# Sixteen attention heads: both value products moved out of the loop over score blocks into runs of 32 matmuls, and half of the layer norm's transpose copies moved to VectorE

## The chip, the cores and the metric

One Trainium2 chip, all 8 cores. Every core runs the same program on its own part of the data, and no core waits for another. The metric is the device time in microseconds of the slowest core. Names of engines: PE is TensorE (its matmuls; PEld its weight loads), DVE is VectorE, ACT is ScalarE, POOL is GpSimd, SP is SyncE.

## The reference, cut to what matters

```python
xn = _layernorm(x)                                  # x: (4, 2048, 2048)
w = (xn @ W.T).reshape(B, T, 16, 128)               # 16 heads of 128
q = _rms_norm(w, g1); k = _rms_norm(w, g2); v = _rms_norm(w, g3)
att = einsum('bhid,bhjd->bhij', q, k) / sqrt(128)
score = softmax(att, axis=-1) + softmax(att, axis=-2)
y = einsum('bhij,bhjd->bihd', score, v)
s = y @ W
g = _silu(_ffn(xn))          # silu(xn@w_gate*s_gate) * (xn@w_up*s_up) @ w_down * s_down
x = x + s * g
```

A core computes 1024 of the 2048 output rows of one batch entry, and needs all 2048 rows as keys and values. Queries, keys and values are one matrix (`rn`, the normalised projection), so the scores are symmetric but for the scales.

## The kernel before, in words

The program is a list of operations for each engine, written out in Python by `Sched.add` (`A` in the code). An engine works off its list in the order written. Each operation counts up a semaphore lane, and `M` reads the count so far, so that a later operation can wait for it. All engines but PE also wait, before each operation, until their own operation before it has ended; an operation of the list may hold many instructions, and between those nothing is waited for. Barriers divide the program into stages.

Stage 1, projection (0 to about 437 us). For each of 16 blocks `tb` of 128 rows: `emit_ln_tr` computes the layer norm (ACT and small DVE operations), `emit_tr` transposes the block by matmuls with the identity matrix, in four groups `grp` of four 128x128 pieces, which alternate between PSUM banks 4 and 5 (L233), and copies each group to SBUF on ACT (L242, L247); `emit_wproj` multiplies by W in two halves of 32 matmuls of 512 columns (L265), and each half is squared by ACT (L276), summed by DVE (L282), turned into a factor by ACT (L288, L292) and scaled into `rn` by DVE (L299). The order in the list is: layer norm of `tb`, projection of `tb-1`, transposes of `tb`.

Stage 2, heads (about 438 to 1625 us), the loop over `h` from L329. For each of 16 heads:

- ACT makes three small vectors of exponentials of the running shift `nMu` (`eMb`, `eMf`, `eNg`: L330, L334, L337).
- PE transposes the head's slice of `rn` (L346, 16 pieces in 4 groups), ACT copies it to `rnT` (L358), DVE scales it to `rnTq` (L362) and makes `vv2`, the values scaled by `eMf`, in 16 instructions (L365).
- The loop over 16 row blocks `rb` (L400). `a_block` computes scores (L383): two matmuls of 512 columns for `rb` below 8, and for `rb` from 8 on two for the low half and two for the high half. ACT takes the exponential of 1024 columns into `Ei[rb]` (L419), and from `rb` 8 on of the high half into a scratch tile (L425), which is needed for its sum alone. PE adds `vv2[rb]` times `Ei[rb]` to the first value product, Y1 (L443, two matmuls).
- In the same loop PE works on the second value product, Y2, of the head before (`pend`): L405, two matmuls a round, which read `Ei[rb]` of that head. There is one `Ei`, so the exponential of the round, which overwrites `Ei[rb]`, waits for them (the list `ew`, L416 to L418). At the end DVE adds Y1 and Y2 (L457) and stores the head (L460).
- After the loop: a logarithm on ACT (L463), the column sums (L470, 64 matmuls of one column), eight small DVE operations (L478 to L490) that end in the reciprocals `rS` and the column factors `fbf`, then `vv1`, the values scaled by `rS`, as 16 single operations (L495), and the factors spread over all partitions: eight small matmuls (L502), a copy to a row (L508), two matmuls (L512, L514), a copy (L518), and the product with Y1 (L521).

After the last head, Y2 of head 15 is done by itself, 32 matmuls in a row (L545), and added and stored (L554, L556).

Stage 3 (1625 us to the end): multiplication by W (L585), then the two feed-forward passes (L658, L664, L723) with weights that stream from memory.

PSUM in stage 2: Y1 in columns 0 to 1023, score buffers at 1024 and 3072, the high half at 3072, Y2 at 2048.

Of the kernel before, what the change touches and what calls it, by code (L numbers as in the profile page):

```python
# [51 lines left out]
def build(debug=False):  # L52
# [95 lines left out]
    A = sch.add  # L148
# [34 lines left out]
    trv_done = [0, 0, 0, 0]  # L183
# [41 lines left out]
    def emit_tr(tb):  # L225
        bi, bj = tb % 3, tb % 2
        for grp in range(4):
            bank = 4 + (grp % 2)
            def tfn(t, tb=tb, bj=bj, grp=grp, bank=bank):
                last = None  # L230
                for kk in range(4):
                    k = grp * 4 + kk
                    last = t.matmul(  # L233
                        PS[:, bank * 512 + kk * 128: bank * 512 + (kk + 1) * 128],
                        xn_t[bj][:, 128 * k:128 * (k + 1)], ident[:, :],
                        start=True, stop=True)
                return last
            A("T", tfn, 1, [("S", ln_xn_mark[bi]), ("S", trv_done[2 * (grp % 2)])])
            tg = M("T")
            if tb < 8:  # L240
                def vfn(v, tb=tb, grp=grp, bank=bank):
                    return v.copy(  # L242
                        xnT_lo[:, 4 * grp:4 * (grp + 1), 128 * tb:128 * (tb + 1)],
                        PS[:, bank * 512:(bank + 1) * 512])
            else:
                def vfn(v, bj=bj, grp=grp, bank=bank):
                    return v.copy(  # L247
                        xnT_t[bj][:, 4 * grp:4 * (grp + 1), :],
                        PS[:, bank * 512:(bank + 1) * 512])
            A("S", vfn, 1, [("T", tg), ("T", xnTt_user[bj] if tb >= 8 else 0)])  # L250
            trv_done[2 * (grp % 2)] = M("S")
        tr_done[bj] = M("T")
        trv_all_t[tb] = M("S")

    def emit_wproj(tb):
        for fh in range(2):
            slot = (2 * tb + fh) % 2
            pofs = slot * 1024
            for k in range(16):
# [11 lines left out]
                kw = [("S", trv_all_t[tb]), ("V", pw_user[slot])] if k == 0 else []  # L271
# [52 lines left out]
    prev_tcs = 0  # L324
    prev_tft = 0
    prev_y1c15 = 0
    pend = None
    trv = [0, 0]
    for h in range(NH):  # L329
        A("S", lambda s: s.activation(eMb[:, :], nMu[:, :], AF.Exp, bias=0.0,  # L330
                                      scale=consts[:, C_NEG1:C_NEG1 + 1]), 1,
          [("V", prev_s1war), ("T", prev_tcs)])
        semb = M("S")
        A("S", lambda s: s.activation(eMf[:, :], nMu[:, :], AF.Exp, bias=0.0,  # L334
                                      scale=consts[:, C_NEG1:C_NEG1 + 1]), 1)
        semf = M("S")
        A("S", lambda s: s.activation(eNg[:, :], nMu[:, :], AF.Exp, bias=0.0,  # L337
                                      scale=1.0), 1)
        seng = M("S")
        for grp in range(4):  # L340
# [24 lines left out]
        A("V", lambda v, h=h: [v.tensor_scalar_mul(  # L365
            vv2[:, rb, :], rn[:, rb, 128 * h:128 * (h + 1)],
            eMf[:, rb:rb + 1]) for rb in range(16)][-1], 1,
          [("S", semf), ("T", prev_y1c15)])
        vvv2 = M("V")

        def a_block(rb, lo, ws):
            if rb < 8:
                pofs = 1024 if rb % 2 == 0 else 3072
                nr = (0, 1)
            elif lo:
                pofs, nr = 1024, (0, 1)
# [12 lines left out]
            A("T", afn, 1, ws)  # L389
            return M("T")  # L390

        amark_lo = {}
        amark_hi = {}
        amark_lo[0] = a_block(0, True, [("V", vq)])
        amark_lo[1] = a_block(1, True, [("V", vq), ("V", prev_fbcV)])
        exp_mark = {}
        exp_done = {}
        y1c_mark = {}
        cur_y2c = {}
        for rb in range(16):  # L400
            if pend is not None:
                def yfn(t, hp=pend["h"], rb=rb):
                    last = None
                    for n in range(2):
                        last = t.matmul(  # L405
                            PS[:, 2048 + 512 * n:2048 + 512 * (n + 1)],
                            vv1[:, rb, :], Ei[:, rb, 512 * n:512 * (n + 1)],
                            start=(rb == 0), stop=(rb == 15))
                    return last
                ws = [("V", pend["vv1m"][rb])]  # L410
                if rb == 0:
                    ws += [("V", pend["fbcV"]), ("S", trv[0])]
                A("T", yfn, 1, ws)
                cur_y2c[rb] = M("T")
            slot = 1024 if (rb >= 8 or rb % 2 == 0) else 3072
            ew = [("T", amark_lo[rb])]  # L416
            if pend is not None:
                ew.append(("T", cur_y2c[rb]))  # L418
            A("S", lambda s, rb=rb, slot=slot: s.activation(  # L419
                Ei[:, rb, :], PS[:, slot:slot + 1024], AF.Exp,  # L420
                bias=nMu[:, rb:rb + 1], scale=1.0,
                accum_out=S1[:, rb:rb + 1]), 1, ew)
            exp_mark[rb] = M("S")
            if rb >= 8:
# [15 lines left out]
            def y1fn(t, rb=rb):  # L440
                last = None
                for n in range(2):
                    last = t.matmul(PS[:, 512 * n:512 * (n + 1)],  # L443
                                    vv2[:, rb, :],
                                    Ei[:, rb, 512 * n:512 * (n + 1)],
                                    start=(rb == 0), stop=(rb == 15))
                return last
            y1w = [("S", exp_mark[rb]), ("V", vvv2)]
            if rb == 0:
                y1w.append(("V", prev_scY1))  # L450
            A("T", y1fn, 1, y1w)
            y1c_mark[rb] = M("T")
            if rb >= 8 and rb <= 14:
                amark_hi[rb + 1] = a_block(rb + 1, False,
                                           [("S", exp_done[rb])])
            if pend is not None and rb == 15:
                A("V", lambda v: v.tensor_tensor(  # L457
                    scY2[:, :], scY1[:, :], PS[:, 2048:3072], ALU.add), 1,
                  [("T", cur_y2c[15])])
                A("V", lambda v, hp=pend["h"]: v.tensor_scalar_mul(  # L460
                    y_st[:, hp, :], scY2[:, :], gv[:, 3:4]), 1)
                prev_scY2 = M("V")
# [13 lines left out]
        A("T", csfn, 1, [("S", semb), ("S", exp_done[15]), ("V", prev_scY2)])  # L476
        tcs = M("T")
        A("V", lambda v: v.tensor_sub(nM[:, :], nMu[:, :], nM[:, :]), 1,  # L478
          [("S", sln)])
        A("V", lambda v: v.tensor_scalar_min(nMu[:, :], nM[:, :], 0.0), 1)  # L480
        A("V", lambda v: v.tensor_copy(cs_sb[:, :], PS[:, 2560:2568]), 1,
          [("T", tcs), ("S", seng)])
# [383 lines left out]
```

How the kernel before makes its waits and increments, by code:

```python
        def emit(eng_name, eng):  # L779
            last_wait = {k: 0 for k in Sched.LANES}
            done = {k: 0 for k in Sched.LANES}
            for (fn, inc, waits, lane) in sch.ops[eng_name]:
                ws = list(waits)
                if lane != "T" and done[lane] > last_wait[lane]:
                    ws.append((lane, done[lane]))
                for (we, wv) in ws:
                    if wv > last_wait[we]:
                        eng.wait_ge(sems[we], wv)
                        last_wait[we] = wv
                if fn is None:
                    inst = eng.nop()
                else:
                    inst = fn(eng)
                if inc:
                    inst.then_inc(sems[lane], inc)
                done[lane] += inc
```

## Time and profile before

| | us |
|---|---|
| two runs of the kernel | 3539.60 and 3624.77 |
| their median | 3582.19 |
| the profiled execution, device time | 3539.33 |
| its span, slowest core (core 1) | 3537.8 |
| spans of the other cores | 3520.1 to 3534.3 |
| mean granted TensorE clock, all cores | 0.884 to 0.887 of 2.4 GHz |

The profile is of one execution, on its slowest core. The span runs from the core's first to its last instruction; the device time is 1.5 us longer. The two medians of the dies are 3533.1 and 3529.8 us. The clock takes two values in the records of all eight cores, 0.5 and 1.0 of full speed (1.2 and 2.4 GHz). The page divides the span into 40 slices of 88 us; stage 2 fills slices 5 to 18. The durations of matmuls are modelled, and reach a little past the start of the next.

### The profile page before, as it was taken

The page shows a single profiled execution, that of the slowest core. Times are in us where ns is not written, and L with a number is a line of the kernel's source. Part 1 is how long each engine was busy: PE and PEld are TensorE (multiplying, and loading weights), DVE is VectorE, ACT ScalarE, POOL GpSimd, SP SyncE. Part 2 cuts the span into 40 slices and gives each one's busy share as a digit, 9 for nine tenths or more (in the row PEclk, how much of TensorE's full clock was granted, in tenths as well). Part 3 has the DMA queues.
Part 4 walks back from the last instruction along what each step waited for, and adds up shares of the span by engine and source line. Part 5 has one row for each costly group of instructions (what it writes and reads, how often), then busy time and mean ns, then how long its engine had stood idle before and what let it go on. Part 6 is the DMA issues. An engine that isn't in the chain of part 4 may idle for free.

```text
span 3537.8 us, 30050 instructions; the slowest of 8 cores (3520.1 to 3537.8 us)
## 1 busy us (share of the span) xinstructions
PE 2445.0 (69%) x11176; PEld 1014.5 (29%) x11176; DVE 587.4 (17%) x1171; ACT 821.4 (23%) x1306; POOL 138.2 (4%) x222
## 2 busy tenths in 40 slices
PE   2777755445554454544989999775768999976565
PEld 0333311111111111111434444322223444422222
DVE  0222211221111221111112222001002122200101
ACT  2555454444444344440000011000000101100000
POOL 0000000000000000000000000010110000001010
PEclk9888888878888778886989999998898999989898
DMA  7111000000000000005034433355554334345543
GB/s 155 42 42 48 1 1 0 1 1 0 1 1 1 1 0 1 0 1 95 36 156 168 164 143 143 143 179 197 182 202 167 143 143 160 126 177 179 202 178 143
DMA packets 56305, 329.20 MB, mean 93 GB/s; under 512 B 4961, under 2 KB 4961, under 8 KB 43873
## 3 DMA queue, kind: packets, MB, share of 16 engines
q0 software_dynamic: 48384, 285.23, 23.1%
q1 hardware_dynamic: 7778, 42.05, 3.4%
q8 instruction: 91, 1.49, 0.2%
q14 instruction: 52, 0.43, 0.0%
HBM read 197.24 MB, written 12.58 MB: 59 GB/s over the span
## 4 chain that ended last, share of the span: by engine, by line
PE 48%; DMA 23%; ACT 15%; issue 7%; DVE 5%; ACTq 0%; DVEq 0%; POOLq 0%; POOL 0%; SPq 0%; PEldq 0%
DMA wdb<-wd_in 19%; PE PS L658 13%; PE PS L664 12%; ACT Ei L419 9%; PE PS L265 7%; PE PS L383 5%; PE PS L405 4%; ACT escr L425 3%; PE PS L585 3%; DVE vv L495 2%; DMA whT<-wt_in 2%; PE PS L443 2%; PE PS L470 1%; ACT rnT L358 1%; DMA ws_lo<-ws_in 1%
## 5 line engine op out<-in xcount | busy, mean ns | idle before, releaser
L723 PE MATMUL PS<-wdb,fuse 128*128 128x512 bf16 x2048 | 535.1, 421 | 273.0 <-DMA wdb<-wd_in 248.8
L383 PE MATMUL PS<-rnT,rnTq 128*128 128x512 bf16 x768 | 250.2, 414 | 405.0 <-ACT Ei L419 345.1
L658 PE MATMUL PS<-xnT_lo,wgb 128*128 128x512 bf16 x2048 | 467.5, 382 | 23.5 <-DVE outs_t L754 19.4
L664 PE MATMUL PS<-xnT_lo,wub 128*128 128x512 bf16 x2048 | 462.9, 379 | 0.0
L419 ACT ACTIVATE Ei<-PS,nMu 128x1024 bf16<-128x1024 f32 x256 | 285.0, 1113 | 445.8 <-PE PS L405 442.2
L723 PEld LDWEIGHTS PS<-wdb,fuse 128*128 128x128 bf16 x2048 | 208.9, 106 | 599.2 <-issue 429.3
L658 PEld LDWEIGHTS PS<-xnT_lo,wgb 128*128 128x128 bf16 x2048 | 201.4, 98 | 270.1 <-issue 31.6
L677 ACT ACTIVATE guscr<-PS,sgv 128x512 f32<-128x512 f32 x128 | 87.9, 687 | 797.2 <-PE PS L664 797.2
L664 PEld LDWEIGHTS PS<-xnT_lo,wub 128*128 128x128 bf16 x2048 | 200.3, 98 | 241.7
L383 PEld LDWEIGHTS PS<-rnT,rnTq 128*128 128x128 bf16 x768 | 52.6, 99 | 598.9 <-issue 598.9
L682 DVE TENSOR_SCALAR guscr<-PS,suv 128x512 f32<-128x512 f32 x128 | 96.1, 751 | 697.9 <-ACT guscr L677 697.9
L746 ACT ACTIVATE outs_t<-scrA 128x2048 f32<-128x2048 f32 x8 | 15.3, 1909 | 819.5 <-DVE scrA L736 819.5
L443 PE MATMUL PS<-Ei,vv 128*128 128x512 bf16 x512 | 164.5, 405 | 23.2 <-ACT Ei L419 23.2
L265 PE MATMUL PS<-whT,xnT_lo 128*128 128x512 bf16 x512 | 136.2, 433 | 44.2 <-DMA whT<-wt_in 36.1
L405 PE MATMUL PS<-Ei,vv 128*128 128x512 bf16 x480 | 162.1, 423 | 0.0
L457 DVE TENSOR_TENSOR scY<-scY,PS 128x1024 f32<-128x1024 f32 x15 | 18.3, 1221 | 794.4 <-PE PS L405 794.4
L736 DVE TENSOR_TENSOR scrA<-PS,sd_bc 128x2048 f32<-128x2048 f32 x8 | 18.3, 2292 | 766.8 <-PE PS L723 766.4
L425 ACT ACTIVATE escr<-PS,nMu 128x1024 bf16<-128x1024 f32 x128 | 142.5, 1113 | 12.4 <-ACT Ei L419 0.7
L265 PE MATMUL PS<-whT,xnT_t 128*128 128x512 bf16 x512 | 129.8, 421 | 8.2 <-ACT xnT_t L247 8.2
L710 POOL DMA_DIRECT2D wdb<-wd_in x128 | 91.3, 713 | 807.5 <-DMA wdb<-wd_in 643.1
L685 DVE TENSOR_TENSOR fuse<-guscr,guscr 128x512 bf16<-128x512 f32 x128 | 88.7, 693 | 13.3
L265 PEld LDWEIGHTS PS<-whT,xnT_lo 128*128 128x128 bf16 x512 | 53.8, 107 | 124.5 <-issue 79.4
(93 smaller groups left out, 1313.1 us busy)
## 6 DMA issues: line engine op xcount, KB each, us to landing
wdb<-wd_in POOLq DMA_DIRECT2D x128, 1024.0 KB, 5.3
wgb<-wg_in POOLq DMA_DIRECT2D x32, 2048.0 KB, 7.5
wub<-wu_in POOLq DMA_DIRECT2D x32, 2048.0 KB, 11.8
x_t<-x_in SPq DMA_DIRECT2D x16, 1024.0 KB, 5.2
whT<-wt_in POOLq DMA_DIRECT2D x8, 1024.0 KB, 15.6
xr_t<-x_in SPq DMA_DIRECT2D x8, 1024.0 KB, 7.2
out<-outs_t SPq DMA_DIRECT2D x8, 1024.0 KB, 4.0
ws_lo<-ws_in POOLq DMA_DIRECT2D x4, 1024.0 KB, 12.2
```

Source lines behind the costliest of these rows:

```text
L265: last = t.matmul(PS[:, pofs + 512 * n: pofs + 512 * (n + 1)], lhsT, whT[:, k, 1024 * fh + 512 * n: 1024 * fh + 512 * (n + 1)], start=(k = ...
L383: last = t.matmul(PS[:, pofs + 512 * n: pofs + 512 * (n + 1)], rnTq[:, 128 * rb:128 * (rb + 1)], rnT[:, 512 * n:512 * (n + 1)], start=True ...
L405: last = t.matmul(PS[:, 2048 + 512 * n:2048 + 512 * (n + 1)], vv1[:, rb, :], Ei[:, rb, 512 * n:512 * (n + 1)], start=(rb == 0), stop=(rb = ...
L419: A("S", lambda s, rb=rb, slot=slot: s.activation(Ei[:, rb, :], PS[:, slot:slot + 1024], AF.Exp, bias=nMu[:, rb:rb + 1], scale=1.0, accum_ ...
L425: A("S", lambda s, rb=rb: s.activation(escr[:, :], PS[:, 3072:4096], AF.Exp, bias=nMu[:, rb:rb + 1], scale=1.0, accum_out=S2[:, rb:rb + 1] ...
L443: last = t.matmul(PS[:, 512 * n:512 * (n + 1)], vv2[:, rb, :], Ei[:, rb, 512 * n:512 * (n + 1)], start=(rb == 0), stop=(rb == 15))
L585: last = t.matmul(PS[:, pofs + 512 * n:pofs + 512 * (n + 1)], lhsT, rhs_t[:, fc % 8, 512 * n:512 * (n + 1)], start=(fc == 0), stop=(fc == 15))
L658: last = t.matmul(PS[:, pg:pg + 512], wgb[wbi][:, k, 128 * ib:128 * (ib + 1)], xnT_lo[:, k, 512 * sp:512 * (sp + 1)], start=(k == 0), stop ...
L664: last = t.matmul(PS[:, pu:pu + 512], wub[wbi][:, k, 128 * ib:128 * (ib + 1)], xnT_lo[:, k, 512 * sp:512 * (sp + 1)], start=(k == 0), stop ...
L682: A("V", lambda v, col=col, pu=pu, gp=gp: v.tensor_scalar_mul(guscr2[gp][:, :], PS[:, pu:pu + 512], suv[:, col:col + 1]), 1, [("T", tgu), ...
L710: A("G", lambda g, r=r, wbi=wbi: g.dma_start(out=wdb[wbi][:, :, :], in_=wd_in[256 * r:256 * (r + 1), :].rearrange("(u p) c -> p u c", u=2) ...
L723: last = t.matmul(PS[:, pofs + 512 * n:pofs + 512 * (n + 1)], fuse[:, ic, 256 * tp + 128 * tb2:256 * tp + 128 * (tb2 + 1)], wdb[wbi][:, u, ...
```

## The change

Three things are done.

Stage 1. The copies of transposed groups 1 and 3 go from ACT to DVE (`e.tensor_copy`); groups 0 and 2 stay on ACT. PE's wait for a free bank, and the projection's wait for the transposed block, name the lane of the engine that copied.

Stage 2, the loop over row blocks. It holds only scores and exponentials. Y2 of the head before is gone from it, and with it the wait of each exponential for those matmuls; `pend` is gone, and the flush behind the last head. Y1 is gone from it too. Score blocks have two buffers in PSUM columns 0 to 2047 for `rb` below 8 (0 and 1024), and two of 2048 columns (0 and 2048) from `rb` 8 on, where low and high half are one group of four matmuls; block `rb` waits for the exponential of block `rb-2`, block 8 for that of block 7.

Stage 2, after the loop, in the order written: the three small exponentials and the logarithm (ACT), the column sums (PE, now in bank 7), `vv2` (DVE), Y1 as one run of 32 matmuls, the small DVE operations, `vv1` as one operation of 16 instructions, the eight small matmuls, the row copy, the two spreading matmuls, and Y2 of the same head as one run of 32 matmuls into columns 1024 to 2047, with the addition and the store. The next head's transposes stand behind that run on PE.

The core of the diff ("..." where lines are left out):

```diff
-    trv_done = [0, 0, 0, 0]
+    trv_done = [("S", 0), None, ("V", 0), None]
...
+            ev = "S" if grp % 2 == 0 else "V"
...
+                    return e.tensor_copy(dst, src_) if ev == "V" else e.copy(dst, src_)
+            A(ev, vfn, 1, [("T", tg), ("T", xnTt_user[bj] if tb >= 8 else 0)])
+            trv_done[2 * (grp % 2)] = (ev, M(ev))
...
-            if pend is not None:
-                def yfn(t, hp=pend["h"], rb=rb):
-                    last = None
-                    for n in range(2):
-                        last = t.matmul(
-                            PS[:, 2048 + 512 * n:2048 + 512 * (n + 1)],
-                            vv1[:, rb, :], Ei[:, rb, 512 * n:512 * (n + 1)],
-                            start=(rb == 0), stop=(rb == 15))
-                    return last
...
-            ew = [("T", amark_lo[rb])]
-            if pend is not None:
-                ew.append(("T", cur_y2c[rb]))
...
+                pofs = ((rb - 8) % 2) * 2048
+                width = 2048
+                if rb == 8:
+                    war = [("S", exp_done[6]), ("S", exp_done[7])]
...
+        A("V", vv2fn, 1, [("S", semf)])
...
+        def y1fn(t, h=h):
+            last = None
+            for rb in range(16):
+                for n in range(2):
+                    last = t.matmul(PS[:, 512 * n:512 * (n + 1)],
+                                    vv2[:, rb, :], Ei[:, rb, 512 * n:512 * (n + 1)],
+                                    start=(rb == 0), stop=(rb == 15))
+            return last
+        A("T", y1fn, 1, [("V", vvv2), ("S", sexp_all)])
...
-        for rb in range(16):
-            vw = [("T", cur_y2c[rb])] if pend is not None else []
-            A("V", lambda v, rb=rb, h=h: v.tensor_scalar_mul(
+        def vv1fn(v, h=h):
+            last = None
+            for rb in range(16):
+                last = v.tensor_scalar_mul(vv1[:, rb, :],
+                                           rn[:, rb, 128 * h:128 * (h + 1)],
+                                           rS[:, rb:rb + 1])
+            return last
+        A("V", vv1fn, 1)
...
+        A("T", y2fn, 1, [("V", vvv1)])
```

PE, the last two rounds of a head and the turn to the next, before. `L383` are scores, `L443` is Y1 (`vv_73` is `vv2`), `L405` is Y2 of the head before (`vv_72` is `vv1`), `L470` the column sums, `L502` to `L514` the factors, `L346` the transposes of the next head:

```order
L383 MATMUL PS<-rnT,rnTq 128x512 x2
L443 MATMUL PS<-Ei,vv_73 128x512 x2
L383 MATMUL PS<-rnT,rnTq 128x512 x2
L405 MATMUL PS<-Ei,vv_72 128x512 x2
L443 MATMUL PS<-Ei,vv_73 128x512 x2
L470 MATMUL PS<-eMb,Ei 128x1 x64
L502 MATMUL PS<-ident,fbf 1x128 x8
L512 MATMUL PS<-frow,ones_107 128x512
L514 MATMUL PS<-frow,ones_107 128x512
L346 MATMUL PS<-ident,rn 128x128 x16
L383 MATMUL PS<-rnT,rnTq 128x512 x4
```

PE, a whole head, after. `L379` are scores, `L439` Y1, `L492` Y2, `L418` the column sums, `L468` to `L479` the factors, `L337` the transposes of the next head:

```order
L379 MATMUL PS<-rnT,rnTq 128x512 x48
L418 MATMUL PS<-eMb,Ei 128x1 x64
L439 MATMUL PS<-Ei,vv_73 128x512 x32
L468 MATMUL PS<-ident,fbf 1x128 x8
L477 MATMUL PS<-frow,ones_107 128x512
L479 MATMUL PS<-frow,ones_107 128x512
L492 MATMUL PS<-Ei,vv_72 128x512 x32
L337 MATMUL PS<-ident,rn 128x128 x16
```

The number of matmuls in a head is the same, 48 and 32 and 32 of 512 columns; the two value products have left the stretch in which the scores stand.

ACT, the end of one projection block in stage 1, before (`L276` to `L292` the factors of the second half, `L247` the four copies of the transposed block, `L196` the next layer norm):

```order
L276 ACTIVATE PS<-PS 128x1024
L288 ACTIVATE rsv<-rmsS,consts 128x8
L292 ACTIVATE rsv<-rsv,consts 128x8
L247 CAST xnT_t_68<-PS 128x512 x4
L196 ACTIVATE xsq,lnst<-x_t_64 128x2048
```

DVE at the same place, after (`L283` the sum and `L300` the scaling of a half, `L250` the copies of groups 1 and 3, `L203` the next layer norm):

```order
L283 TENSOR_REDUCE rmsS<-PS 128x8
L300 TENSOR_TENSOR rn<-PS,rsv 128x1024
L283 TENSOR_REDUCE rmsS<-PS 128x8
L300 TENSOR_TENSOR rn<-PS,rsv 128x1024
L250 CAST xnT_t_69<-PS 128x512 x2
L203 TENSOR_SCALAR lnst<-lnst 128x1
```

On ACT two of the four copies are left at that place; on DVE the other two stand behind the scaling of the second half.

## Rows read from the trace of the kernel before

**Rows 1.** The page: the span, and the chain that ended last, by line.

```profile
span 3537.8 us, 30050 instructions; the slowest of 8 cores (3520.1 to 3537.8 us)
...
DMA wdb<-wd_in 19%; PE PS L658 13%; PE PS L664 12%; ACT Ei L419 9%; PE PS L265 7%; PE PS L383 5%; PE PS L405 4%; ACT escr L425 3%; PE PS L585 3%; DVE vv L495 2%; DMA whT<-wt_in 2%; PE PS L443 2%; PE PS L470 1%; ACT rnT L358 1%; DMA ws_lo<-ws_in 1%
```

**Rows 2.** Stage 2: length; busy PE, PEld, DVE, ACT, POOL; PEclk, DMA share, GB/s.

```profile
437.70:1625.00 1187.30, 599.50 (x3232) 223.38 (x3232) 236.37 (x752) 516.75 (x896) 0.00 (x0) 0.82 0.00 1
```

**Rows 3.** Who waited for whom: microseconds in total, times, the longest.

```profile
ACT Ei L419 <- PE PS L405: 442.2, 240, 3.9
```

**Rows 4.** Timeline, a round below 8 and two starts from 8 on: start, us, engine, line.

```profile
738.13 1.11 ACT L419 ACTIVATE Ei<-PS,nMu 128x1024 bf16<-128x1024 f32 x1 [1.75 <-PE PS L405]
...
739.48 0.59 PE L383 MATMUL PS<-rnT,rnTq 128*128 128x512 bf16 x2 [1.50 <-ACT Ei L419]
...
740.34 0.59 PE L405 MATMUL PS<-Ei,vv 128*128 128x512 bf16 x2
...
741.08 1.11 ACT L419 ACTIVATE Ei<-PS,nMu 128x1024 bf16<-128x1024 f32 x1 [1.75 <-PE PS L405]
...
751.68 1.11 ACT L419 ACTIVATE Ei<-PS,nMu 128x1024 bf16<-128x1024 f32 x1 [1.32 <-PE PS L405]
...
755.50 1.11 ACT L419 ACTIVATE Ei<-PS,nMu 128x1024 bf16<-128x1024 f32 x1 [1.32 <-PE PS L405]
```

**Rows 5.** Timeline of head 0, first exponential to the logarithm after the last.

```profile
443.89 1.11 ACT L419 ACTIVATE Ei<-PS,nMu 128x1024 bf16<-128x1024 f32 x1 [2.24 <-PE PS L383]
...
445.24 1.01 PE L383 MATMUL PS<-rnT,rnTq 128*128 128x512 bf16 x2 [0.65 <-ACT Ei L419]
...
475.01 0.22 ACT L463 ACTIVATE nM<-S 128x16 f32<-128x16 f32 x1
```

**Rows 6.** Timeline from there into head 1.

```profile
475.40 0.18 DVE L478 TENSOR_TENSOR nM<-nMu,nM 128x16 f32<-128x16 f32 x1 [30.02 <-ACT nM L463]
...
478.79 0.31 ACT L330 ACTIVATE eMb<-nMu,consts 128x16 bf16<-128x16 f32 x1 [3.56 <-DVE fcol L487]
...
479.01 1.01 PE L502 MATMUL PS<-ident,fbf 128*1 128x128 bf16 x8 [2.21 <-DVE fbf L490]
...
484.86 1.21 DVE L508 CAST frow<-PS 1x1024 bf16<-1x1024 f32 x1
486.21 0.58 PE L512 MATMUL PS<-frow,ones 1*128 1x512 bf16 x1 [6.19 <-DVE frow L508]
...
487.15 1.03 PE L346 MATMUL PS<-ident,rn 128*128 128x128 bf16 x8
...
491.66 2.69 DVE L365 TENSOR_SCALAR vv<-rn,eMf 128x128 bf16<-128x128 bf16 x16
491.70 1.87 PE L383 MATMUL PS<-rnT,rnTq 128*128 128x512 bf16 x4 [1.81 <-DVE rnTq L362]
```

**Rows 7.** Timeline of the end of stage 2.

```profile
1613.52 9.17 PE L545 MATMUL PS<-Ei,vv 128*128 128x512 bf16 x32 [1.54 <-DVE f_bc L518]
1622.86 1.22 DVE L554 TENSOR_TENSOR scY<-scY,PS 128x1024 f32<-128x1024 f32 x1 [8.16 <-PE PS L545]
```

**Rows 8.** Granted clock by stretch (PEclk, third from the end), as rows 2.

```profile
744.00:772.70 28.70, 14.89 (x58) 4.60 (x58) 1.78 (x2) 18.68 (x31) 0.00 (x0) 1.00 0.00 1
...
792.90:801.30 8.40, 5.44 (x12) 1.49 (x12) 0.00 (x0) 2.41 (x4) 0.00 (x0) 0.50 0.00 0
...
474.50:477.70 3.20, 1.74 (x64) 1.68 (x64) 0.85 (x5) 0.64 (x3) 0.00 (x0) 1.00 0.02 5
```

**Rows 9.** Timeline of stage 1, end of one block.

```profile
253.87 2.60 ACT L247 CAST xnT_t<-PS 128x512 bf16<-128x512 f32 x4
253.95 1.23 DVE L299 TENSOR_TENSOR rn<-PS,rsv 128x1024 bf16<-128x1024 f32 x1 [1.10 <-ACT rsv L292]
...
255.27 0.38 PE L233 MATMUL PS<-ident,xn_t 128*128 128x128 bf16 x4 [0.29 <-ACT xnT_t L247]
...
256.73 16.91 PE L265 MATMUL PS<-whT,xnT_t 128*128 128x512 bf16 x64 [1.07 <-ACT xnT_t L247]
```

More of the change, by code:

```diff
@@ L317, in build @@
         sch.barrier()
+    head_tail_V = 0
+    head_tail_S = 0
+    prev_csV = 0
     prev_fbcV = 0
+    prev_y2T = 0
     prev_exp15 = 0
@@ L323, in build @@
     prev_scY2 = 0
[L324 to L327, printed above, removed]
     trv = [0, 0]
     for h in range(NH):
[L330 to L339, printed above, removed]
         for grp in range(4):
@@ L440, in y1fn @@
[L440 to L462, printed above, removed]
+        sexp_all = M("S")
@@ L463, in build @@
+        A("S", lambda s: s.activation(eMb[:, :], nMu[:, :], AF.Exp, bias=0.0,
+                                      scale=consts[:, C_NEG1:C_NEG1 + 1]), 1)
+        semb = M("S")
+        A("S", lambda s: s.activation(eMf[:, :], nMu[:, :], AF.Exp, bias=0.0,
+                                      scale=consts[:, C_NEG1:C_NEG1 + 1]), 1)
+        semf = M("S")
+        A("S", lambda s: s.activation(eNg[:, :], nMu[:, :], AF.Exp, bias=0.0, scale=1.0), 1)
+        seng = M("S")
         A("S", lambda s: s.activation(nM[:, :], S1[:, :], AF.Ln,
@@ L475, in csfn, with vv2fn @@
             return last
-        A("T", csfn, 1, [("S", semb), ("S", exp_done[15]), ("V", prev_scY2)])
+        A("T", csfn, 1, [("S", semb)])
         tcs = M("T")
[L478 to L481, printed above, removed]
+        def vv2fn(v, h=h):
+            last = None
+            for rb in range(16):
+                last = v.tensor_scalar_mul(vv2[:, rb, :],
+                                           rn[:, rb, 128 * h:128 * (h + 1)],
+                                           eMf[:, rb:rb + 1])
+            return last
+        A("V", vv2fn, 1, [("S", semf)])
+        vvv2 = M("V")
+        def y1fn(t, h=h):
+            last = None
+            for rb in range(16):
+                for n in range(2):
[4 more added lines that the diff above has]
+        A("T", y1fn, 1, [("V", vvv2), ("S", sexp_all)])
+        ty1 = M("T")
+        A("V", lambda v: v.tensor_copy(cs_sb[:, :], PS[:, 3584:3592]), 1,
           [("T", tcs), ("S", seng)])
+        csV = M("V")
         A("V", lambda v: v.tensor_mul(cs_sb[:, :], cs_sb[:, :], eNg[:, 0:8]), 1)
```

171 lines of the change are left out of this document (70 added, 101 removed).

## The prediction

> **What bounds the kernel now.** I read the page first. The chain that ended last spreads over three stages [rows 1]: the feed-forward lines (wdb, L658, L664) hold the most, and the heads appear as L419, L383, L405, L425 and L443, together about a quarter. The change touches only the projection and the heads, so I cut out the heads' stage by its barriers: 1187.3 us, in which ACT is busy for 516.8, PE for 599.5, DVE for 236.4 [rows 2]. No engine is full. It is a stage of waits, and the list of waits names one above all others: ACT's exponential into Ei waits 442.2 us, 240 times, for L405, the second value product of the head before [rows 3]. That is 15 heads times 16 rounds, so every round of every head but the first.
>
> The timeline shows the ring [rows 4]. An exponential starts at 738.13; PE starts the score pair 1.35 later, when it and its sum have ended; the Y1 pair and the Y2 pair follow, the Y2 pair at 740.34; the next exponential starts at 741.08, 0.15 behind that pair's end. A round is 2.95 us, of which ACT works 1.30. From row block 8 on, with two exponentials a round, it is 3.82 (751.68 to 755.50). Sixteen rounds are 8 x 2.95 + 8 x 3.82 = 54.2 us. Head 0 has no Y2 to do, and shows the same loop without the ring: from its first exponential (443.89) to the logarithm behind the last (475.01) 31.1 us, which is 24 exponentials of 1.30 with nothing between them [rows 5]. The loop that was written to overlap two heads runs as a chain: exponential, scores, Y1, Y2, exponential.
>
> **The change, head by head.** The loop then costs what head 0 shows, and both products come behind it, in the open. I sum one head, from exponential 0 to the next head's exponential 0.
>
> 1. 24 exponentials: 31.1 us [rows 5].
> 2. Block 8 needs both buffers, so its four score matmuls start only behind exponential 7. At half clock 1.87 [rows 6], with 0.05 before (1.35 less 1.30) and 0.15 behind [rows 4]: 2.1. A matmul of 512 columns takes 0.215 at full clock (four of them from 739.48 to 740.34) and 0.43 at half (four in 1.87, two in 1.01) [rows 4 to 6]. At full clock two steps of 0.215 and a pair's 0.59 make 1.0, so the item 1.2.
> 3. To the start of Y1. Three small exponentials (0.31 for eMb and for eMf, 0.22 as the logarithm for eNg, 0.09 between them) now stand ahead of the logarithm, 1.1; the subtraction starts 0.39 behind the logarithm's start [rows 5, 6]; it and the minimum take 0.55; then vv2, 2.69 [rows 6], which was hidden beside the scores and now is in the open; 0.15 to PE (486.07 to 486.21). Together 4.9. The column sums lie beside vv2.
> 4. Y1, 32 matmuls. The flush behind the last head is that run, from a rested PE: 9.17 us [rows 7]. All at full clock it would be 31 x 0.215 + 0.38 = 7.0. I take 9.2.
> 5. From Y1 to Y2. The small DVE operations and vv1 end beside Y1: at most 3.6 (475.40 to 479.01, with the column sums in it) and, as one operation like vv2, 2.7, against 9.2. What is left is a chain that Y1 now holds up on PE: eight small matmuls (1.01 at half clock, about 0.65 at full), 0.15, row copy to L512 1.35 (484.86 to 486.21), two matmuls until PE is free again 0.94 (to 487.15), 0.45 at full [rows 6]. 2.6 at full clock, 3.45 at half. I take 2.6.
> 6. Y2: 7.0 if the clock holds over step 5, 9.2 if not. I take 7.0.
> 7. Transposes of the next head to its first score matmul: 487.15 to 491.70, 4.55, with a rested PE [rows 6]. The store of the head lies beside them on DVE (1.22 + 0.75 and gaps against 3.6). Behind a dense run the first pieces are faster: 4.3.
> 8. First pair to exponential 0: 1.01 + 0.15 [rows 5, 4] at half clock, 0.75 at full: 1.0.
>
> Sum: 31.1 + 2.1 + 4.9 + 9.2 + 2.6 + 7.0 + 4.3 + 1.0 = 62.2 us.
>
> The stage: 6.2 from its start to the first exponential (437.70 to 443.89), 15 heads of 62.2, then 56.9 (items 1 to 6), and 2.2 for addition and store (1622.86 to 1625.00) [rows 2, 5, 7]. 6.2 + 933.0 + 56.9 + 2.2 = 998.3, against 1187.3: 189 us less.
>
> **Which clock.** Items 2, 4, 5, 6 hang on it. In rounds with 58 matmuls in 28.7 us (2.0 a us) it stayed at 2.4 GHz; in rounds at a head's start with 12 in 8.4 us (1.4 a us) it stayed at 1.2 [rows 8]. The new loop issues two a 1.30 us, 1.5 a us, nearest to the second row. So scores at half clock, and Y1 starts there. For Y2 the nearest row is 474.50 to 477.70: full clock for 3.2 us in which PE did only one-column work [rows 8]. Step 5 is shorter and has ten larger matmuls in it, so Y2 starts at full clock.
>
> At half clock a pair takes 1.01 [rows 5], so scores end 0.05 + 1.01 + 0.15 = 1.21 us behind the exponential two before, under the 1.30 that the one between takes. Scores stay hidden, with 0.1 to spare.
>
> The Trainium skill has a rule that speaks against the new shape ("TensorE: Matmul & The Clock Gate", section "A second HAM failure mode: psum-queue depth-cycling"): a matmul kernel that cycles through PSUM banks with short idles between its groups swings between half and full clock, and pays for it in throughput. Rows 8 agree that both levels occur within one head. Carried to this kernel at its worst, it would leave Y1 and Y2 at half clock too; that case is priced below from rows, as the rival "half clock throughout".
>
> **The projection.** ACT's first copy stands behind the factors of the half before, and starts at 253.87; its four copies end at 256.47, the next projection starts at 256.73 [rows 9]. DVE's two copies stand behind the scaling of that half, which ends at 255.18. I have no row of DVE copying 128x512 to SBUF; 1024 columns took 1.21 in the row copy [rows 6], so half of that, 0.61, to 1.21; with a fixed part I take 0.69. Then 255.28 + 0.69, group 3 on PE (0.14 + 0.38 [rows 9]), its copy 0.14 + 0.69, and 0.26 to the projection: 257.6, 0.8 later than now. Blocks 1 to 15 pay that: 12 us. Bounds: from -9, if the copies ran beside each other and DVE's scaling were no hindrance, to +25, at 1.21 a copy.
>
> **The sum**, against the profiled execution's own time: 3539.3 - 189 + 12 = 3362 us. The median of the two runs shown is 3582.2; the profiled execution agrees with the faster of them (3539.6), and I predict for such a run.
>
> **Rivals.**
>
> - *The clock stays up in the loop.* Items 2, 4, 8 fall by 0.9, 2.2, 0.3: 3.4 a head, 55 us: 3307. For it: head 0 ran at full clock in its loop. Against it: that loop had Y1 in it.
> - *The clock falls between Y1 and Y2.* Items 5, 6, 7 rise by 0.85, 2.2, 0.25: 3.3 a head, 53 us: 3415. For it: PE does little in step 5. Against: the 3.2 us of rows 8.
> - *Half clock throughout* (the rule above at its worst). A run is 32 x 0.43 = 13.7: Y1 +4.5, Y2 +6.7, with the rival before's other 1.1: 12.3 a head, 197 us: 3559, no change. Against it: the flush started rested, and its 9.17 us show that the clock rose inside the run.
> - *The exponentials wait for their scores* (the slower side). If a score group does not run while ACT reads the other buffer, or comes too late for it, each exponential waits for its whole group: 1.2 for a pair, 2.0 for four. 8 x 1.2 + 7 x 2.0 = 23.6 a head, 378 us: 3740. It decides from 11.1 us a head (177 / 16), 0.7 per group. Against it: head 0 had these buffers and 1.30 a round, even in its first rounds at half clock.
> - *The change does not do what it says*: the instruction order shows 48 score matmuls in a row and no value product between them, so I give this nothing.
>
> **How the numbers follow.** Forecast 0.62, clock up 0.12, clock down between the runs 0.17, half clock throughout 0.06, late scores 0.03. The likeliest is 3362. The range runs from the first rival's 3307 to 3425, the second's with 10 us of the projection's bound: about 0.9. A measurement of this kernel tells about 2 per cent from no change, which is 71 us. The first three cases are faster by more: 0.91. Half clock throughout is within it: 0.06. Late scores: 0.03 slower.
>
> **What would show it.** Right: no wait of the exponential for a Y2 matmul; 1.30 from one exponential to the next, a gap of 2 us only at block 8; a head in 62 us; stage 2 near 1000 us. The runs of 32: Y1 near 9.2, Y2 near 7.0, at clock 1.00 in Y2. The projection stage about 450 us instead of 437.7. Stage 3 unchanged at 1913 us. Wrong: exponentials with idle time before each, released by score matmuls; a run of 32 that takes 13 us; stage 2 above 1115 us.

## The result, and the profile after

| | us |
|---|---|
| changed kernel, median of 11 runs | 3374.69 |
| its lowest, and the profiled execution | 3354.96, 3354.6 |
| kernel before, median of 10 runs | 3539.77 |
| ratio | 0.9505, 95% interval 0.947 to 0.954 |

Forecast were 3362 us and a range of 3307 to 3425. Some runs of this program have one die or both at a lower clock and take some per cent longer; the ratio leaves them out, while the median of 11 holds three of them, and three at 3375 to 3395, above the five at 3355 to 3357. I set the steps against the profiled execution, as the sum was.

The three stages of the slowest core (columns: length; busy PE, PEld, DVE, ACT, POOL with counts; PEclk, DMA share, GB/s):

```profile
0.00:454.50 454.50, 291.45 (x1280) 126.77 (x1280) 112.63 (x162) 181.44 (x241) 7.23 (x22) 0.88 0.23 56
454.50:1441.60 987.10, 656.47 (x3232) 232.11 (x3232) 213.85 (x752) 517.11 (x896) 0.00 (x0) 0.69 0.00 1
1441.60:3352.70 1911.10, 1550.95 (x6664) 664.50 (x6664) 260.50 (x290) 104.51 (x137) 130.94 (x200) 0.93 0.44 159
```

The heads went from 1187.3 us [rows 2] to 987.1, 200 less (forecast 189). Stage 1 is 16.8 longer (forecast 12). Stage 3 is the same, 1911 for 1913. ACT is as busy in the heads as before, 517 us; PE's figure rose from 600 to 656 at the same 3232 matmuls, since more of them ran at half clock (0.69 granted, for 0.82).

In the list of waits, 442.2 us of ACT waiting for Y2 [rows 3] are gone. What is left of that kind:

```profile
ACT Ei L387 <- PE PS L379: 65.6, 32, 2.2
PE PS L439 <- DVE vv L429: 41.8, 16, 2.9
```

The first is two waits a head, the head's first exponential and block 8. The second is Y1's wait for vv2 in the open, 2.6 us a head.

The timeline of one head, from exponential 0 on (compare [rows 4 to 6]; L379 scores, L439 Y1, L492 Y2, L429 vv2, L337 transposes):

```profile
522.21 1.11 ACT L387 ACTIVATE Ei<-PS,nMu 128x1024 bf16<-128x1024 f32 x1 [1.87 <-PE PS L379]
...
523.51 1.11 ACT L387 ACTIVATE Ei<-PS,nMu 128x1024 bf16<-128x1024 f32 x1
523.56 1.01 PE L379 MATMUL PS<-rnT,rnTq 128*128 128x512 bf16 x2 [1.13 <-ACT Ei L387]
...
524.80 1.11 ACT L387 ACTIVATE Ei<-PS,nMu 128x1024 bf16<-128x1024 f32 x1
...
534.66 1.11 ACT L387 ACTIVATE Ei<-PS,nMu 128x1024 bf16<-128x1024 f32 x1 [2.16 <-PE PS L379]
...
555.42 0.31 ACT L400 ACTIVATE eMb<-nMu,consts 128x16 bf16<-128x16 f32 x1
...
557.75 2.69 DVE L429 TENSOR_SCALAR vv<-rn,eMf 128x128 bf16<-128x128 bf16 x16
```

From one exponential to the next 1.30, the score pair 1.01 long (half clock) beside it; block 8 stands alone with 2.16 of idle; from the first exponential to the small ones 33.2. The head before it, from vv2 on, shows the rest:

```profile
495.98 2.69 DVE L429 TENSOR_SCALAR vv<-rn,eMf 128x128 bf16<-128x128 bf16 x16
...
498.82 8.87 PE L439 MATMUL PS<-Ei,vv 128*128 128x512 bf16 x32 [2.60 <-DVE vv L429]
...
500.76 2.69 DVE L459 TENSOR_SCALAR vv<-rn,rS 128x128 bf16<-128x128 bf16 x16
...
507.62 0.61 PE L468 MATMUL PS<-ident,fbf 128*1 128x128 bf16 x8
508.40 1.21 DVE L474 CAST frow<-PS 1x1024 bf16<-1x1024 f32 x1 [4.95 <-PE PS L468]
...
510.28 7.08 PE L492 MATMUL PS<-Ei,vv 128*128 128x512 bf16 x32
...
517.20 0.61 PE L337 MATMUL PS<-ident,rn 128*128 128x128 bf16 x8
```

Two runs of 32 equal matmuls, 8.87 and 7.08 us. vv1 (L459) is made beside the first run, and behind it DVE waits 4.95 us for PE.

The place in stage 1 that answers to [rows 9]:

```profile
261.66 1.22 DVE L300 TENSOR_TENSOR rn<-PS,rsv 128x1024 bf16<-128x1024 f32 x1 [1.11 <-ACT rsv L293]
262.31 0.38 PE L233 MATMUL PS<-ident,xn_t 128*128 128x128 bf16 x4 [3.86 <-ACT xnT_t L250]
262.84 0.59 ACT L250 CAST xnT_t<-PS 128x512 bf16<-128x512 f32 x1 [0.67 <-PE PS L233]
262.99 0.69 DVE L250 CAST xnT_t<-PS 128x512 bf16<-128x512 f32 x1
...
263.82 0.58 PE L233 MATMUL PS<-ident,xn_t 128*128 128x128 bf16 x4 [1.14 <-DVE xnT_t L250]
264.59 0.69 DVE L250 CAST xnT_t<-PS 128x512 bf16<-128x512 f32 x1 [0.91 <-PE PS L233]
...
265.43 3.15 PE L266 MATMUL PS<-whT,xnT_t 128*128 128x512 bf16 x7 [1.01 <-DVE xnT_t L250]
```

From the scaling's start to the next projection it is 3.8 us, and was 2.8 in [rows 9].

### The profile page after: what moved, and what is told of

It is laid out like the page before. It is cut to its first block, busy times and chain, and to the rows that moved or that the text cites. A ratio compares the mean times of both kernels' runs of the same rounds, so it can differ in the third digit from the quotient of the medians.

```text
span 3352.7 us, 29493 instructions; the slowest of 8 cores (3340.2 to 3352.7 us)
## 1 busy us (share of the span) xinstructions
PE 2498.9 (75%) x11176; PEld 1023.4 (31%) x11176; DVE 587.0 (18%) x1203; ACT 803.1 (24%) x1274; POOL 138.2 (4%) x222
## 3 DMA queue, kind: packets, MB, share of 16 engines
q0 software_dynamic: 48384, 285.23, 24.5%
## 4 chain that ended last, share of the span: by engine, by line
PE 48%; DMA 25%; ACT 15%; issue 7%; DVE 6%; ACTq 0%; DVEq 0%; POOLq 0%; POOL 0%; PEldq 0%; SPq 0%
DMA wdb<-wd_in 20%; PE PS L615 13%; PE PS L621 13%; ACT Ei L387 9%; PE PS L266 8%; PE PS L439 4%; PE PS L492 3%; ACT escr L394 3%; PE PS L542 3%; DMA whT<-wt_in 2%; DVE vv L429 1%; PE PS L379 1%; ACT rnT L349 1%; PE PS L680 1%; DMA ws_lo<-ws_in 1%
## 5 line engine op out<-in xcount | busy, mean ns | idle before, releaser
L379 PE MATMUL PS<-rnT,rnTq 128*128 128x512 bf16 x768 | 337.7, 580 | 186.4 <-ACT escr L394 89.3
L379 PEld LDWEIGHTS PS<-rnT,rnTq 128*128 128x128 bf16 x768 | 74.5, 118 | 438.0 <-issue 430.8
L439 PE MATMUL PS<-Ei,vv 128*128 128x512 bf16 x512 | 138.7, 438 | 41.8 <-DVE vv L429 41.8
L349 ACT CAST rnT<-PS 128x512 bf16<-128x512 f32 x64 | 37.5, 586 | 341.6 <-PE PS L337 337.6
L492 PE MATMUL PS<-Ei,vv 128*128 128x512 bf16 x512 | 113.3, 379 | 0.0
L233 PE MATMUL PS<-ident,xn_t 128*128 128x128 bf16 x256 | 26.0, 244 | 104.4 <-ACT xnT_t L250 30.9
```

The source lines that it names most:

```text
L379: last = t.matmul(PS[:, pofs + 512 * n: pofs + 512 * (n + 1)], rnTq[:, 128 * rb:128 * (rb + 1)], rnT[:, 512 * n:512 * (n + 1)], start=True ...
L439: last = t.matmul(PS[:, 512 * n:512 * (n + 1)], vv2[:, rb, :], Ei[:, rb, 512 * n:512 * (n + 1)], start=(rb == 0), stop=(rb == 15))
L492: last = t.matmul(PS[:, 1024 + 512 * n:1024 + 512 * (n + 1)], vv1[:, rb, :], Ei[:, rb, 512 * n:512 * (n + 1)], start=(rb == 0), stop=(rb = ...
```

## The experiments

Times are the lowest of each kernel's runs; the kernel before had 3534 to 3537 as its lowest beside them. Ratios are to the kernel before, on the same chip. Where two kernels are compared by a stage, the length is read from the traces: the heads' stage agrees between the eight cores of a trace within 4 us, mostly within 2, while the whole time also holds what the other stages vary by. That matters most for e2, e3 and e6, whose times rest on one or two runs.

### Each part of the change alone

`e1_copies_only` is the kernel before with the diff of stage 1; `e2_heads_only` the changed kernel without it:

```diff
-    trv_done = [("S", 0), None, ("V", 0), None]
+    trv_done = [0, 0, 0, 0]
...
-            ev = "S" if grp % 2 == 0 else "V"
...
-            A(ev, vfn, 1, [("T", tg), ("T", xnTt_user[bj] if tb >= 8 else 0)])
+            A("S", vfn, 1, [("T", tg), ("T", xnTt_user[bj] if tb >= 8 else 0)])
```

> The kernel before, with the change of stage 1 alone (transposed groups 1 and 3 copied by DVE). Theory: DVE's copies stand behind its scaling of the second half, which delays each block from 1 to 15 by 0.8 us as forecast, or by 1.1 as stage 1 of the changed kernel suggests (454.5 us for 437.7): 3552 to 3557 us in all. Rival: the copies run beside each other and the longer stage 1 is chance: 3540 or less.

> The changed kernel with stage 1 as before (all four copies on ACT). Theory: stage 1 back to 438 us, heads unchanged at 987 us, 3338 us in all. Rival: the two parts act on each other, or stage 1 is longer for another reason: 3355 us.

Measured: e1 3552.6 (ratio 1.0058, 1.0038 to 1.0078), e2 3338.1. The parts add up. The first head's transposes start at 439 us on average over the cores in the kernel before and in e2, and at 455 in e1 and in the changed kernel: stage 1 costs 16 us in either surrounding. The heads' stage is 986 us in e2 and 987 in the changed kernel, 1189 in e1 and 1187 before: about 200 us less, whatever stage 1 does.

### Why a block of stage 1 is longer

`e9_scaling_behind` leaves the copies on DVE and emits the scaling of the second half after them:

```diff
-            A("V", rnfn, 1, [("S", srs)])
-            pw_user[slot] = M("V")
+            def put(rnfn=rnfn, srs=srs, slot=slot):
+                A("V", rnfn, 1, [("S", srs)])
+                pw_user[slot] = M("V")
+            if fh == 1:
+                return put
+            put()
...
         if tb < NTB:
             emit_tr(tb)
+        if tb >= 1:
+            put()
```

> The changed kernel with DVE's scaling of the second half put behind the transpose copies in stage 1. Theory (the 1.1 us a block are the place of DVE's two copies behind that scaling): each block 1.4 us shorter, stage 1 at 433 us for 454.5, 3334 us for 3355. Rival (a DVE copy is slow in itself, or DVE and ACT hinder each other): stage 1 stays above 445 us, 3347 or more.

Measured: 3327.5, 27 less than the changed kernel (ratio 0.9406, 0.9387 to 0.9424). The transposes of head 0 start at 430.6. DVE copies the first group before ACT has its factors ready:

```profile
250.41 0.69 DVE L250 CAST xnT_t<-PS 128x512 bf16<-128x512 f32 x1
...
252.84 0.69 DVE L250 CAST xnT_t<-PS 128x512 bf16<-128x512 f32 x1 [1.74 <-PE PS L233]
...
253.64 1.23 DVE L300 TENSOR_TENSOR rn<-PS,rsv 128x1024 bf16<-128x1024 f32 x1
```

The copy takes the same 0.69 us. Its place cost the time, not the engine: stage 1 is about 8 us shorter than in the kernel before when DVE's copies stand ahead of the scaling (431 us for 439, means of the cores), and 16 longer when they stand behind it.

### What held the loop before

`e4_ring_no_wait` leaves all matmuls in the loop of the kernel before, in their order, and takes away why the exponential had to wait. Y2 reads `xnT_lo` in place of `Ei`; so this kernel computes another Y2.

```diff
-                            vv1[:, rb, :], Ei[:, rb, 512 * n:512 * (n + 1)],
+                            vv1[:, rb, :], xnT_lo[:, rb, 512 * n:512 * (n + 1)],
...
-            if pend is not None:
-                ew.append(("T", cur_y2c[rb]))
```

> The kernel before, with the Y2 matmuls in the loop where they were, but reading xnT_lo in place of Ei (so Y2 and the output are other numbers), and so without the wait of the exponential for them. Theory (the wait, not the work): PE has 3 pairs of 0.43 us to do in a round of 1.30 us of ACT, so rounds of 1.3 to 1.5 below block 8 and 2.6 from there, a loop of 33 us in place of 54: 15 x 21 us less, 3220 us in all. Rival (PE's work and its order hold the loop, the wait adds nothing): rounds near 2.9 and 3.8 us as before, 3450 us or more.

Measured: 3170.0, 364 less than the 3533.7 of the kernel before beside it; the heads' stage is 821 us for 1187. With three pairs of matmuls a round, the exponentials run one behind the other (L417; L441 is Y1, L405 Y2):

```profile
655.08 1.11 ACT L417 ACTIVATE Ei<-PS,nMu 128x1024 bf16<-128x1024 f32 x1
655.33 0.59 PE L383 MATMUL PS<-rnT,rnTq 128*128 128x512 bf16 x2
655.76 0.59 PE L441 MATMUL PS<-Ei,vv 128*128 128x512 bf16 x2
656.19 0.59 PE L405 MATMUL PS<-xnT_lo,vv 128*128 128x512 bf16 x2
656.38 1.11 ACT L417 ACTIVATE Ei<-PS,nMu 128x1024 bf16<-128x1024 f32 x1
```

A round of 1.30 us where [rows 4] have 2.95, and the same work. So the wait was the cause, and PE's load was not. It is 50 us less than my 3220, because I had both loops wrong. From the first exponential to the logarithm, the 15 heads with a Y2 take 55.3 us on average in the kernel before (53.0 to 57.6; I had 54.2) and 31.9 in e4 (I had 33). That is 23.4 us a head and not 21, and 1.1 more are saved between the logarithm and the next head's first exponential (18.6 us for 19.7): 15 x 24.5 = 367 us, and the stage is 366 shorter.

`e3_y2_run` takes the wait away with the result kept: only Y2 leaves the loop, Y1 and vv2 stay in it. vv1 is one operation here, as in the changed kernel.

```diff
-            if pend is not None:
-                def yfn(t, hp=pend["h"], rb=rb):
...
-                ew.append(("T", cur_y2c[rb]))
...
+        A("V", vv1fn, 1)
...
+        A("T", y2fn, 1, [("V", vvv1)])
+        ty2 = M("T")
```

> The kernel before, with Y2 alone taken out of the loop and done as a run of 32 at the end of its own head; Y1 stays in the loop and vv2 ahead of it. Theory (the wait of the exponential for Y2 held the loop): the loop takes 31.1 us in every head as in head 0, and behind it 1.9 (column sums) + 1.9 (small operations) + 2.7 (vv1) + 2.6 (factors) + 9.2 (Y2) + 5.4 to the next exponential: 55 us a head, 3233 us in all. Rival (Y1 in the loop holds it as well, both had to leave): a loop of over 38 us, no faster than the heads of the changed kernel, 3338 us or more.

Measured: 3222.5 (ratio 0.9123, 0.9101 to 0.9145). That is 116 less than e2, which has the same stage 1 and differs in that Y1 and vv2 have left the loop too, and in its score buffers, which make the gap at block 8. Of the 116, 109 are in the heads' stage (877 us for 986), 7 a head. Y1 cost next to nothing in the loop, since it fits beside the exponentials: 31.9 us from the first exponential to the logarithm, where 24 exponentials of 1.30 make 31.2. The loop of a head and the Y2 run behind it (granted clock third from the end):

```profile
936.61:968.59 31.98, 22.60 (x78) 6.67 (x76) 1.92 (x12) 28.91 (x48) 0.00 (x0) 0.89 0.00 0
977.64:986.32 8.68, 8.68 (x36) 3.69 (x36) 2.45 (x2) 0.00 (x0) 0.00 (x0) 0.81 0.00 0
```

The loop is at 0.89 here, and at 0.50 to 0.57 in the changed kernel. The run behind it has nothing of that: over the 16 heads it takes 8.1 to 8.9 us from its first to its last matmul, where 6.7 is full clock (Y2 of the changed kernel). Between the two lie 9 us with the column sums and the small matmuls alone.

### How much of the gain is vv1

In the kernel before, vv1 is 16 operations with a wait between each two. `e10_vv1_one_op` changes that alone:

```diff
-            A("V", lambda v, rb=rb, h=h: v.tensor_scalar_mul(
-                vv1[:, rb, :], rn[:, rb, 128 * h:128 * (h + 1)],
-                rS[:, rb:rb + 1]), 1, vw)
-            vv1m.append(M("V"))
+        A("V", vv1fn, 1, [("T", cur_y2c[15])] if pend is not None else [])
+        vv1m = [M("V")] * 16
```

> The kernel before, with vv1 made in one operation of 16 instructions in place of 16 operations that each wait for the one before. Theory: vv1 takes 2.7 us in place of 5.7, and the factors' row copy behind it comes 3.0 us earlier in each of 16 heads: 48 us less, 3491 us. So 48 of the 187 us of the heads would come from this edit and the rest from the loop. Rival (the row copy's lateness is hidden by what follows): 3535 us.

Measured: 3483.6 (ratio 0.9826, 0.9746 to 0.9905), some 50 us less, as expected. The interval is wide; the heads' stage is clearer, 1133 to 1137 us over the cores for 1187, and vv1 takes 2.7 us for 5.7. So as much as a quarter of the heads' 200 us was to be had in the kernel before by packing 16 instructions into one operation, with the loop left as it was.

It does not follow that a quarter of the 200 us comes from this edit, as my expectation had it. In the changed kernel vv1 lies beside Y1 and DVE then waits 4.95 us, so 3.0 us more of vv1 would be hidden there by these rows (a version of it with 16 operations was not run). In e3, where vv1 is in the open, the packing counts.

### vv2, and the clock of the two runs

`e5_vv2_early` puts vv2 back beside the scores:

```diff
+        A("V", vv2fn, 1, [("S", semf)])
+        vvv2 = M("V")
         exp_done = [0] * 16
...
-        A("V", vv2fn, 1, [("S", semf)])
-        vvv2 = M("V")
```

> The changed kernel with eMf and vv2 made at the head's start, beside the scores, as before the change. Theory (item 3 of the sum: vv2 lies in the open): Y1 starts behind the column sums, 2.4 us behind the last exponential in place of 4.9, and the small operations follow earlier: 2.5 x 16 = 40 us less than the changed kernel, 3315 us for its 3355. Rival (the column sums or the small operations on DVE take vv2's place as what Y1 or the factors wait for): under 10 us, 3345 or more.

Measured: 3337.8 (ratio 0.9436, 0.9419 to 0.9452), 17 less and not 40, of which 10 to 13 are in the heads' stage. It is neither value. Y1 does start earlier, 2.2 us behind the last exponential in place of 4.9; but from its first to its last matmul it now takes 9.2 us on average (8.3 before, core 5), and Y2 7.9 (6.7). The head is 60.8 us for 61.5. More than half of what the earlier start brought went into matmuls at half clock, and that of Y2 I had not thought of. Grouped by line, e5's Y1 (L440) and Y2 (L493); the third number is the mean of one matmul in ns, 438 and 379 in the changed kernel:

```profile
L440 PE MATMUL PS<-Ei,vv 128*128 128x512 bf16 x512 | 153.4, 474 | 0.0
L493 PE MATMUL PS<-Ei,vv 128*128 128x512 bf16 x512 | 133.0, 426 | 0.0
```

The heads do not agree: on this core four of the 16 have Y2 at 6.7 us and the others at 8.1 to 8.4.

`e6_filler` tests the clock by itself: 12 matmuls ahead of the column sums and 5 behind them, whose results Y1 overwrites.

```diff
+        def filla(t):
+            last = None
+            for i in range(12):
+                last = t.matmul(PS[:, 512 * (i % 2):512 * (i % 2 + 1)],
+                                rnTq[:, 0:128], rnT[:, 0:512],
+                                start=True, stop=True)
+            return last
+        A("T", filla, 1, [("S", exp_done[14])])
```

> The changed kernel with 17 matmuls a head that change no result (12 before the column sums, 5 behind them, into the columns that Y1 then overwrites), so that PE is dense before Y1. Theory (Y1's 8.8 us for Y2's 7.1 are the clock): Y1 takes 7.1 at clock 1.00, 1.7 x 16 = 27 us less, 3328 us. Rival (Y1 is longer for what it reads, or for its place): Y1 stays at 8.8 and the run at 3355 or more.

Measured: 3358.2, no gain (heads' stage 986 to 987 us, as in the changed kernel); and yet the theory of the clock holds. The two products, grouped by line: first the changed kernel (L439 Y1, L492 Y2), then e6 (L455 Y1, L508 Y2); columns are busy us, mean ns, idle before.

```profile
L439 PE MATMUL PS<-Ei,vv 128*128 128x512 bf16 x512 | 138.7, 438 | 41.8 <-DVE vv L429 41.8
L492 PE MATMUL PS<-Ei,vv 128*128 128x512 bf16 x512 | 113.3, 379 | 0.0
```

```profile
L508 PE MATMUL PS<-Ei,vv 128*128 128x512 bf16 x512 | 138.5, 439 | 0.0
L455 PE MATMUL PS<-Ei,vv 128*128 128x512 bf16 x512 | 113.1, 379 | 2.7 <-DVE vv L437 2.3
```

They have changed places. Y1 at full clock ends 1.6 us earlier, and now it is Y2 that is 1.6 longer. It does not start at half clock. The clock falls inside it, 0.9 us after its first matmul, and comes back 3.4 us later:

```profile
510.00:510.88 0.88, 0.88 (x6) 0.41 (x6) 0.64 (x1) 0.00 (x0) 0.00 (x0) 1.00 0.00 0
510.88:514.30 3.42, 3.42 (x10) 1.18 (x9) 1.81 (x2) 0.00 (x0) 0.00 (x0) 0.50 0.00 0
514.30:518.60 4.30, 4.30 (x21) 1.95 (x20) 0.00 (x0) 0.00 (x0) 0.00 (x0) 1.00 0.00 0
```

That is, nearly, the second rival of the prediction, which the changed kernel escapes in all 16 heads and e6 in one of 16. `e12_filler_both` adds six such matmuls between Y1 and Y2, where PE waits for the row copy:

```diff
+        A("T", fillc, 1, [("S", exp_done[15])])
         vfrow = M("V")
```

> e6 with six more matmuls that change no result between the eight small factor matmuls and the two spreading ones, where PE waits 1.5 us for the row copy. Theory (Y2 is slow in e6 because the clock fell in the gap ahead of it): both runs take 7.1 us, 1.7 x 16 = 27 us less than e6, 3332 us. Rival (filling the gap does not hold the clock, or it costs what it gains): one of the runs stays at 8.8, 3358 us or more.

Measured: 3325.8 (ratio 0.9359, 0.9247 to 0.9471), with both runs at full clock:

```profile
510.51 7.07 PE L455 MATMUL PS<-Ei,vv 128*128 128x512 bf16 x32
517.51 0.61 PE L484 MATMUL PS<-ident,fbf 128*1 128x128 bf16 x8
518.05 1.47 PE L494 MATMUL PS<-rnT,rnTq 128*128 128x512 bf16 x6
```

```profile
L516 PE MATMUL PS<-Ei,vv 128*128 128x512 bf16 x512 | 113.3, 379 | 0.0
L455 PE MATMUL PS<-Ei,vv 128*128 128x512 bf16 x512 | 113.1, 379 | 2.4 <-DVE vv L437 2.3
```

A head is 60.2 us for 61.4 in e6, and the heads' stage 967 us for 986. In the total it is 32 us to e6 and 29 to the changed kernel. So 23 matmuls a head that compute nothing make the heads 20 us faster; the other 9 us lie in the other stages, where nothing was changed (in the profiled executions stage 1 is 12 us longer and stage 3 16 shorter on the slowest core), and are not theirs.

### A version that beats both

`e8_y2_first` starts from e3 (the diff is against the kernel before). vv1 is made in four operations and Y2 runs in four pieces, each as soon as its vv1 is there; the row copy runs beside the first two, the spreading stands behind them. `e11_best` adds the stage 1 of e9.

```diff
+        for g4 in range(4):
...
+            A("V", vv1fn, 1)
             vv1m.append(M("V"))
...
+            A("T", y2fn, 1, [("V", vv1m[g4])])
+            if g4 == 1:
...
+                A("T", fbcfn, 1, [("V", vfrow)])
```

> As e3 (Y1 in the loop, Y2 a run at the end of its head), with vv1 made in four operations and the Y2 run in four pieces, which start as vv1 comes, and the factors' row copy and spreading beside Y2 in place of ahead of it. Theory: Y2 starts 4.9 us behind the last exponential in place of 9, and takes 9.2: 50.5 us a head for 54, 3166 us in all. Rival (the factors on DVE then hold the next head's scaled copy): 54 us a head as e3, 3222 us.

> e8 with the stage 1 of e9 (Y1 in the loop, Y2 a run at its own head's end in four pieces, half of the transpose copies on DVE and ahead of its scaling). Theory: the two stages add up, 3170 less the 10 us by which e9's stage 1 is shorter than that of the kernel before (430.6 for 438.4 to the first transposes of head 0): 3161 us. Rival (they do not add up): 3170 or more.

Measured: e8 3170.9 (ratio 0.9013, 0.8949 to 0.9076), e11 3157.3 (0.8893, 0.8829 to 0.8956; its four runs lie between 3157 and 3164). Against the kernel before it is 11% faster, where the change is 5%. The heads' stage is 821 to 823 us in both, 55 less than e3's (the pieces of Y2 and the place of the row copy were not run apart); in e11 stage 1 is 430 us, as in e9.

## Why the prediction was right

The bound was read rightly: the ring of exponential, scores, Y1, Y2. e4 shows it with only the wait, and what Y2 reads, changed. One head, step by step, measured as the mean over the heads of the slowest core:

| step | forecast | measured |
|---|---|---|
| 1, 2: exponentials and block 8 | 33.2 | 33.3 |
| 3: to Y1 | 4.9 | 4.9 |
| 4: Y1 to the factors | 9.2 | 8.6 |
| 5: factors | 2.6 | 2.7 |
| 6: Y2 | 7.0 | 6.9 |
| 7: to the first scores | 4.3 | 4.3 |
| 8: to exponential 0 | 1.0 | 0.8 |
| head | 62.2 | 61.5 |

The head of 61.5 is the mean of 15, from the column sums' first vector (one in each head, 493.9 to 1416.0):

```profile
L400 ACT ACTIVATE eMb<-nMu,consts x16: 307/307/308, 493.9 to 1416.0; 128x16 bf16<-128x16 f32 x16
```

- The total came out 7 us below the forecast, and that is closer than the parts: the heads took 11 us less than forecast (987 for 998), stage 1 took 5 more and stage 3 2 less.
- Step 1 rested on head 0, which had no Y2. With block 8 it held to 0.3 us in all heads (33.2 to 33.5).
- Step 4 was the flush's 9.17, from a rested PE. Y1 is 0.5 us shorter on average (8.45 to 8.87), since it had less of half clock: 2.8 to 3.7 us of each run, for 4.3 of the flush. Most of the 11 us by which stage 2 beats the forecast is this and step 8.
- Step 6 was the choice that counted most among the unknowns, 2.2 us a head. Full clock was right for this kernel; e6 shows how near the other case was: with a dense PE ahead of Y1, and the same gap ahead of Y2, Y2 took 8.7 to 8.8 us in 15 of 16 heads. My ground for it (3.2 us of weak work at full clock in head 0) was one sample of something that varies, and the runs do not make it a rule. That the value was right is in part luck; had it been wrong, the time would still have been in the range, at the rival's 3415.
- "Scores at half clock, hidden with 0.1 to spare" held: 1.30 a round.
- The rival "half clock throughout" (13.7 us for a run) appeared nowhere; the worst mean was 9.2 from first to last matmul, in e5, and the longest run 9.6.
- The Trainium skill's picture of a clock that swings between its levels ("TensorE: Matmul & The Clock Gate", section "A second HAM failure mode: psum-queue depth-cycling") agrees with this trace, 0.57 granted in the loop and 1.00 in Y2; what it takes here is 1.6 us a head on average, in Y1 (8.3 us from first to last matmul, for Y2's 6.7), not the whole throughput. [rows 8] show the two levels in two neighbouring heads, and not within one as I wrote; but the mean granted clock over a head's loop was 0.86 to 1.00 there, so that most heads had both.
- The term that was too small is the projection's: 1.1 us a block on average, not 0.8. The copy on DVE was 0.69 as estimated. The transposes of group 3, which wait for it longer than before, ran at half clock (0.58 for 0.38), which my step left out. Its lower bound, 9 us less, is near what e9 shows. Its upper bound, worked out again from the same steps, is 28 and not 25; nothing else rests on it.
- Not priced in the forecast: vv1 as one operation in the kernel before, worth 50 us there (e10). I took it as 2.7 us hidden beside Y1, which is right for the new order.

The heads' stages of e3 and e2 say where the change stands: taking Y2 out of the ring and packing vv1 gained 310 us (1187 to 877), taking Y1 and vv2 out of the loop, with the gap at block 8, gave 109 back.

## What to carry to other kernels

Two pipelines over one buffer are one chain if each round of the second overwrites what the first still reads: before trusting an overlap, look for an engine that waits once a round for the same line, and for an iteration (here the first) that runs without it. Take out of the loop only the work that closes the ring; work that fits beside the bound engine is next to free there. It kept TensorE's clock up in the loop itself (0.89 for 0.56), but not for the run that followed 9 us later. Price each part of a change in the order of work in which it will stand: the same edit to vv1 is worth 50 us in the open and, by the rows, nothing beside Y1. A copy given to a less busy engine is worth what its place in that engine's order is worth.

## What the runs showed of the hardware

- The same 32 matmuls took 7.1 us at a granted clock of 1.00 throughout, and 8.5 to 8.9 where it was 0.5 for 2.8 to 3.7 us of the run (Y1 of the changed kernel). The clock at the start does not decide it: e6's Y2 starts at 1.00 and takes 8.8.
- Starting a run 2.7 us earlier made it and the next one longer, by 0.9 and 1.2 us on average (e5). 23 matmuls a head that compute nothing took 20 us off the heads (e12).
- In the loop of scores alone the mean granted clock was 0.57 and a score matmul took 580 ns on average; with Y1 in the loop (e3) it was 0.89 and 410 ns.
- 16 DVE instructions of 128x128 took 5.7 us with a wait for the one before between each two, and 2.7 us as one operation (e10).
- DVE copies 128x512 from PSUM to SBUF as bf16 in 0.69 us, ACT in 0.59.
